# A fused cross-network recommender kernel: the second layer's steps reordered, one subtraction moved, gathers and prelude rearranged

## The reference

```
def _L0_rec_ref(inputs, w0, w1, w2, b0, b1, b2):
    x0 = inputs; xk = inputs; direct = []
    for idx, (W, b) in enumerate([(w0, b0), (w1, b1), (w2, b2)]):
        z = jnp.einsum('bhd,bkd,hks->bsd', x0, xk, W) + b[None, :, None]
        z = jax.nn.relu(z)
        if idx != 2:
            half = z.shape[1] // 2
            xk = z[:, :half, :]
            direct.append(z[:, half:, :])
        else:
            direct.append(z)
    return jnp.sum(jnp.concatenate(direct, axis=1), axis=-1)
...
    h = jnp.concatenate([z, dense_ctx], axis=1)
    h = jnp.maximum(h @ W_top1 + b_top1, 0.0)
    h = jnp.maximum(h @ W_top2 + b_top2, 0.0)
    y = h @ W_top3
```

## Time and profile before

| what | us |
|---|---|
| median of 3 runs | 2593.65 (2592.92 to 2595.34) |
| the profiled execution, its own time | 2598.07 |
| its span, first to last instruction | 2596.2 |
| PE busy | 2443.5 (94%) |
| DVE busy | 2169.6 (84%) |
| POOL busy | 1875.1 (72%) |
| ACT busy | 1661.3 (64%) |

### The profile page before, as it was taken

How to read it: one execution, slowest core, us unless ns; L and a number is a source line. 1 busy time by engine, 2 the same in 40 slices (tenths; PEclk the granted TensorE clock), 3 DMA queues, 4 the chain that set the end, 5 groups by cost and what they waited for, 6 DMA issues and landing times.

```text
span 2596.2 us, 32413 instructions
## 1 busy us (share of the span) xinstructions
PE 2443.5 (94%) x8654; PEld 1591.3 (61%) x8654; DVE 2169.6 (84%) x1872; ACT 1661.3 (64%) x2120; POOL 1875.1 (72%) x1270
## 2 busy tenths in 40 slices
PE   0899999999999999999999999999999999999989
PEld 0466666666656666666666666666666666666655
DVE  1588889889878888988988898898888888888880
ACT  1566666666666666766666676666666666666653
POOL 6578778777867777777787777778777777765450
PEclk6899999999999999999999999999999999999999
DMA  2677667667757766766776676677667666756730
GB/s 71 139 149 155 126 138 166 134 131 151 154 110 152 154 130 132 166 137 132 148 158 129 132 164 140 127 150 155 131 131 166 141 131 145 160 129 129 159 80 0
DMA packets 214715, 352.58 MB, mean 136 GB/s; under 512 B 34382, under 2 KB 47566, under 8 KB 214588
## 3 DMA queue, kind: packets, MB, share of 16 engines
q1 hardware_dynamic: 194717, 347.07, 61.6%
q0 software_dynamic: 19968, 5.15, 2.2%
HBM read 346.97 MB, written 5.12 MB: 136 GB/s over the span
## 4 chain that ended last, share of the span: by engine, by line
POOL 30%; issue 27%; PE 16%; DVE 9%; DMA 7%; ACT 7%; SPq 3%; POOLq 0%; ACTq 0%; DVEq 0%; another core or an unknown queue 0%
POOL emb L374 13%; POOL Pl L380 13%; DMA xb<-x_dram 7%; ACT Ph L514 5%; PE ps L807 5%; PE ps L797 4%; DVE P L692 3%; DVE ps L692 3%; PE ps L817 3%; POOL dir L404 3%; SPq L311 3%; DVE Pl L697 3%; PE ps L926 1%; PE ps L918 1%; POOL emb L385 1%
## 5 line engine op out<-in xcount | busy, mean ns | idle before, releaser
L380 POOL TENSOR_TENSOR Pl<-P,Ph 128x1024 fp32r<-128x1024 f32 x448 | 1072.3, 2397 | 479.1 <-ACT Ph L514 469.4
L692 DVE TENSOR_TENSOR P<-xb,ps 128x1024 f32<-128x1024 f32 x768 | 926.8, 1214 | 81.1 <-DMA xb<-x_dram 72.9
L807 PE MATMUL ps<-Ph,wh 128*128 128x512 f32 x1920 | 870.1, 459 | 8.1 <-ACT Ph L514 8.0
L697 DVE TENSOR_TENSOR Pl<-ps,Ph 128x1024 fp32r<-128x1024 f32 x512 | 626.1, 1223 | 178.9 <-ACT Ph L514 168.7
L374 POOL DMA_INDIRECT emb<-tbl_in,idx x624 | 601.0, 963 | 166.3 <-issue 145.3
L807 PE MATMUL ps<-Ph,wl 128*128 128x512 f32 x1792 | 707.4, 395 | 0.0
L514 ACT ACTIVATE Ph<-ps 128x1024 fp32r<-128x1024 f32 x512 | 523.3, 1022 | 285.3 <-DVE ps L692 217.3
L817 PE MATMUL ps<-Pl,wh 128*128 128x512 f32 x1920 | 689.7, 445 | 11.4 <-POOL Pl L380 11.3
L514 ACT ACTIVATE Ph<-P 128x1024 fp32r<-128x1024 f32 x448 | 474.6, 1059 | 325.3 <-DVE P L692 303.8
L692 DVE TENSOR_TENSOR ps<-xb,ps 128x1024 f32<-128x1024 f32 x512 | 628.2, 1227 | 28.1 <-DMA xb<-x_dram 10.2
L797 PE MATMUL ps<-P,wp 128*128 128x512 f32 x1280 | 603.7, 594 | 4.1 <-DVE P L692 4.1
(11 more groups left out here) (64 smaller groups left out, 826.7 us busy)
## 6 DMA issues: line engine op xcount, KB each, us to landing
xb<-x_dram SPq DMA_DIRECT2D x1280, 256.0 KB, 8.5
emb<-tbl_in,idx POOLq DMA_INDIRECT x624
x_dram<-rows_sb SPq DMA_DIRECT2D x64, 78.0 KB
xb<-w_in SPq DMA_DIRECT2D x15, 128.0 KB
xb<-wt_in SPq DMA_DIRECT2D x2, 512.0 KB, 8.6
xb<-dense_in SPq DMA_DIRECT2D x1, 768.0 KB, 5.9
wp<-w_in SPq DMA_DIRECT2D x5, 128.0 KB
xb<-w0a_in SPq DMA_DIRECT2D x1, 448.0 KB
```

What stands on the lines that cost most here:

```text
L380: pool.tensor_tensor(Pl[:, h_slot(ref, c, k)], P[:, p_slot(ref, c, k)], Ph[:, h_slot(ref, c, k)], ALU.subtract).then_inc(low_pool, 1)
L692: dve.tensor_tensor(p, xb[:, x], xk.unsqueeze(1).broadcast_to([128, 2, N]), ALU.mult)\
L697: dve.tensor_tensor(Pl[:, h_slot(ref, c, k)], p_ps, Ph[:, h_slot(ref, c, k)], ALU.subtract)\
L807: pe.matmul(z_of(c, k), w[:, q, j, :], Ph[:, h_slot(ref, c, k), j, :], start=k in (L1B, L2) and i + j == 0, stop=False)
```

## The change

1. `TURN`: layer 2 takes its pairs in layer 1's order (4 to 9, then 0 to 3), so each slot is used in the same turn by both layers, and SP refills it 10 steps before the next use (before: 6 steps for pairs 4 to 9). The two steps with the single 39th field are now 1 and 11.
2. `KIND`: steps 17 and 19 change kinds; step 17 is G and step 19, the last one, is P.
3. `REST_AT = 19`: DVE subtracts the rest of layer 0 right behind step 19's own work and not after two products of the next chunk; it has a semaphore of its own (`rest_ready`).
4. The gathers are listed step by step (`GATHERS`); the embeddings' full and low parts move from steps 15 and 17 to 17 and 18.
5. Prelude: PE runs 36 matmuls (`WARM`) into a bank that nobody reads, DVE takes `low_emb(0)` from POOL, layer 0's first group uses three banks, the rest form first.
6. The tower's staging tiles are moved to slots that are free earlier.

```diff
-KIND = "GVPVGPVGVPPGVGVGVPVG"
+WARM = 36
+KIND = "GVPVGPVGVPPGVGVGVGVP"
-REST_AT = 1
+REST_AT = 19
-HIGH_AT, FULL_AT, LOW_AT = 15, 15, 17
+HIGH_AT, FULL_AT, LOW_AT = 15, 17, 18
-SINGLE = 2 * PRE + 1
+SINGLE = 2 * PRE + 3
+TURN = [(i + PRE) % PAIRS for i in range(PAIRS)]
-GATHER_AT = [k for k in range(STEPS) if KIND[k] != "G"]
+NEXT_IDS_AT = (2, 0)
+GATHERS = [[1, 2, 3, 5, 9, 14, 16, 18, 19], [1, 2, 3, 5, 6, 8, 9, 10],
+           [1, 2, 3, 5, 6, 9, 10, 12, 14, 16, 18, 19], [1, 2, 3, 5, 6, 8, 9, 10, 18, 19]]
...
+        early_ps = (ps[:, 6, :], ps[:, 7, :], aux_ps, ps[:, 7, :], aux_ps, ps[:, 7, :], aux_ps)
...
-                    for p in range(PAIRS):
+                    for i, p in enumerate(TURN):
-                        sp.wait_ge(products, upto(T, ref, STEP, c, L2 + p))
+                        sp.wait_ge(products, upto(T, ref, STEP, c, L2 + i))
                         spread(c + 2 if p < PRE else c + 1, p)
...
-            low_emb(0)
-            early = 12
+            early = 13
...
-                x = x_slot(c, PRE + k) if k < L1B else x_slot(c + 1, k - L1B) if k < L2 else x_slot(c, k - L2)
+                x = x_slot(c + (L1B <= k < L2), TURN[k % PAIRS])
...
-                dve.tensor_tensor(sqx[LAST_LO, :], aux_ps[LAST_LO], sqx[LAST_LO, :], ALU.subtract).then_inc(aux_read, 1)
+                dve.tensor_tensor(sqx[LOWS, :], bank[LOWS], sqx[LOWS, :], ALU.subtract).then_inc(rest_ready, 1)
+            dve.wait_ge(emb_high, 1)
+            dve.tensor_tensor(emb2[:, :, 1, :], emb[:, :, :].rearrange("p f d -> p d f"),
+                              emb_h[:, :, :].rearrange("p f d -> p d f"), ALU.subtract).then_inc(emb_low, 1)
...
-                        if k == REST_AT and not end and not (first and c == 0):
-                            rest_low(T, c + 1)
+                        if k == REST_AT and not (last and c >= 2):
+                            rest_low(T, c + 2)
...
+            for i in range(WARM):
+                pe.matmul(z1_ps[:, 0], wp[:, 0, 0, :], wp[:, 0:2].rearrange("p q j m -> p (q j m)"), start=True, stop=True)
...
+            transposes(0)
+            pe.wait_ge(aux_read, 1)
+            for i, t in enumerate((FULL0, 0, 1)):
+                sums(t, early_ps[i])
+            for t in range(FULL0):
+                pe.wait_ge(aux_read, 2 + t)
+                contract0(t, 0, t == 0, False)
+                if t + 2 < FULL0:
+                    sums(t + 2, early_ps[t + 3])
+            pe.wait_ge(rest_ready, 1)
+            contract0(FULL0, 0, False, True)
```

More of the change, by code:

```diff
@@ L431, in tile @@
             def tile(T, ref, fields, first=False, last=False):
+                todo = [list(f) for f in fields]
                 for c in range(CPT):
[L434 to L437, removed]
                     for k in range(STEPS):
@@ L440, in tile @@
                             low(T, ref, c, k)
[L441 to L445, removed]
+                        if (c, k) == NEXT_IDS_AT and todo[2]:
+                            next_ids(T + 2)
+                        part = min(c, 1) if (c, k) < NEXT_IDS_AT else 2
+                        n = GATHERS[c].count(k) * (1 + (first and c == 0))
+                        for f in todo[part][:n]:
+                            gather(f)
+                        todo[part] = todo[part][n:]
                         if c == 0 and not first and k in FOLD1_AT:
@@ L463, in tile @@
                             low_emb(T + 1)
-            cuts = (0, 12, 21, 30, NF)
-            third, fourth, first, second = (range(a, b) for a, b in zip(cuts, cuts[1:]))
-            tile(0, 0, (range(early, 30), range(30, NF), third, fourth), first=True)
+            late, soon = len(GATHERS[0]), len(GATHERS[1])
+            cut = NF - late - soon
+            assert sum(map(len, GATHERS)) == NF
+            start, middle, rest = range(0, cut), range(cut, cut + late), range(cut + late, NF)
+            tile(0, 0, (range(early, cut + late), rest, start), first=True)
             with pool.Fori(1, TILES - 2) as T:
-                tile(T, 1, (first, second, third, fourth))
-            tile(TILES - 2, TILES - 2, (first, second, (), ()))
-            tile(TILES - 1, TILES - 1, ((), (), (), ()), last=True)
+                tile(T, 1, (middle, rest, start))
+            tile(TILES - 2, TILES - 2, (middle, rest, ()))
+            tile(TILES - 1, TILES - 1, ((), (), ()), last=True)
             pool.wait_ge(z2_read, chunks)
@@ L537, in _ @@
                 copy_x(0, AUX * g)
-                for t in range(T0):
-                    square(0, AUX * g + 1 + t, t)
-                    s = t - (T0 - PRE - 1)
+                if g:
+                    rest_squares(0, 1, AUX + 1)
+                for t in range(FULL0):
+                    square(0, AUX * g + 2 + t, t, aux_ps if g else early_ps[t + 1])
+                    if t == 0 and not g:
+                        rest_squares(0, 0, 1, early_ps[0])
+                    s = t - (FULL0 - PRE)
                     if g and 0 <= s < PRE and KIND[L1B + s] != "P":
@@ L708, in _ @@
             for s in range(PRE):
+                if s == 1:
+                    rest_low(0, 1)
                 dve.wait_ge(xb_in[s], 32)
@@ L851, in _ @@
             late = None
-            for g in range(2):
-                number = AUX * g
-                if g:
-                    pe.wait_ge(aux_read, number)
-                transposes(g)
-                for t in range(T0):
-                    pe.wait_ge(aux_read, number + 1 + t)
-                    sums(t)
-                    if t:
-                        contract0(t - 1, g)
-                    if g and t >= T0 - PRE:
-                        late = contract(0, 0, -1, L1B + t - (T0 - PRE), late)
-                pe.wait_ge(aux_read, AUX * (g + 1))
-                contract0(T0 - 1, g)
+            transposes(0)
+            pe.wait_ge(aux_read, 1)
+            for i, t in enumerate((FULL0, 0, 1)):
+                sums(t, early_ps[i])
+            for t in range(FULL0):
+                pe.wait_ge(aux_read, 2 + t)
[4 more added lines that the diff above has]
+            contract0(FULL0, 0, False, True)
+            transposes(1)
+            order = (FULL0, *range(FULL0))
+            for i, t in enumerate(order):
+                if i == 1:
+                    pe.wait_ge(rest_ready, 2)
+                else:
+                    pe.wait_ge(aux_read, READS + max(i, 1))
+                sums(t)
+                if i:
+                    contract0(order[i - 1], 1, i == 1, False)
+                if i >= T0 - PRE:
+                    late = contract(0, 0, -1, L1B + i - (T0 - PRE), late)
+            pe.wait_ge(aux_read, 2 * READS)
+            contract0(FULL0 - 1, 1, False, True)
             assert not late
```

74 lines of the change are left out of this document (41 added, 33 removed).

## The result

| what | before | changed |
|---|---|---|
| median of 4 runs | 2593.38 (2592.92 to 2595.34) | 2515.55 (2515.19 to 2517.52) |
| ratio, 95% interval | | 0.970 (0.9683 to 0.9717) |
| the profiled execution's span | 2596.2 | 2514.0 |
| start, up to the loop's first transposes | 100.3 | 97.9 |
| loop, from there to the last transposes (61 chunks) | 2319.4 | 2246.5 |

The changed kernel is 3.0% faster. The transposes run two chunks ahead of the steps, so the last ones stand at the start of the third last chunk; what the tables call the end has three chunks in it. Of the 82.2 us between the two profiled spans the loop has 72.9, the end 6.9 and the start 2.4. The medians differ by 77.8, since the profiled execution of before lay 4.7 us above its median.

The account below looks back on a forecast made before the run. PE was taken to bound the kernel, its gaps being what reordering can win. Terms 71 + 1 + 2 + 5 = 79 us off the 2593.65 us median gave 2515 us; range 2498 to 2547.

Parts of the forecast that it names:

- What bounds the kernel: PE, busy 94% of the span; its largest repeated gap is the wait for DVE at line 789, 55.0 us.
- The subtraction: Behind step 19: moving layer 0's rest subtraction there removes PE's wait, 1.23 us a chunk, 58 times, 71 us.
- The pair order: Layer 2's transfers: 10 steps of lead for 6 keep step 4's inputs on time for an earlier PE; costed at 0.
- rival 1: At step 4: PE meets late rounding or low part, losing about 0.5 us a chunk, 30 us; 2545 us, chance 0.15.
- The gathers: On POOL: three, not five, ahead of step 4's subtraction in chunk c = 1; mostly cover, 2 us (0 to 9).
- The last step plain: Last chunk, step 19 plain and 17 split: ACT rounds one product less ahead of the tower, 1 us (0 to 2).
- The prelude: Before the loop: 1.2 us for the transposes, some 2 for each of two groups; 5 us (0 to 16).
- rivals: The four alternative outcomes to the forecast, which itself had chance 0.66; the range takes in the first two only.
- Which clock: Prelude: added matmuls end at about 54 us, 8 us of nothing follow, half the clock expected at the first group.
- The second gap at step 8: Steps 5 to 8: a chain from PE through ACT ties PE and DVE once a chunk and stays whatever the change does.
- The bounds, 2500 to 2524: The forecast's own limits: prelude 16 or 0, POOL's waits 9 or 0, 58 gaps of 1.0 to 1.3 us.
- 2: Rival on the prelude: the added matmuls do keep the clock, 16 us for 5; 2504 us, chance 0.10.

Follow-up runs that it names:

- a_rest1: The changed kernel with the subtraction of layer 0's rest back at step 1 of the following chunk; 2587.04 us, ratio 0.9963.
- a_kind: The changed kernel with the old kinds of steps 17 and 19 (17 plain, 19 split on POOL); 2521.31 us, ratio 0.9715.
- a_gathers: The changed kernel with gathers as early as possible again, five ahead of step 4 in chunk c = 1; 2528.94 us, ratio 0.9739.
- a_warm0: The changed kernel without the 36 added matmuls of the prelude; 2518.57 us, ratio 0.9698.
- a_warm45: The changed kernel with 45 instead of 36 added matmuls in the prelude; 2514.56 us, ratio 0.9689.
- a_again: The changed kernel run again with nothing changed; 2517.84 us, ratio 0.969.
- a_early22: The changed kernel with 22 instead of 13 gathers ahead of the loop and single gathers in the first chunk; 2521.23 us, ratio 0.9705.

## Why the prediction was right, point by point

The forecast was 2515 us, the measured median 2515.55. The total is that close partly by luck: the largest term is right, and two small ones are off in opposite directions. And the 79 us were worked out on the profiled spans, which moved by 82.2, but taken off the median, which moved by 77.8.

- **What bounds the kernel** (PE's gaps, the one at line 789 first): right. a_rest1 gives the wait back and with it 68.9 us.
- **The subtraction, 1.23 us a chunk, 71 us:** right in the whole. The loop gained 72.9, 1.24 us by the median chunk. The added 0.17 and 0.11 us (hidden idle time, restart) were needed; the recorded 55.0 alone would have fallen short by 16. The spacings of the starts say the same: over 60 chunks of before, those ahead of and behind the contraction at line 789 are 70.2 us longer than two of 0.23 each.
- **The pair order at 0, as cover:** right in kind. It was the step on which most depended, and the runs price it: 28.5 to 30.9 us. I had put about half a us a chunk on losing it in rival 1, and that was the size (30 us).
- **The gathers, mostly cover, 2 us of POOL's waits:** PE's waits for POOL went from 11.3 to 9.9 us, 1.4 us. As cover they are worth up to 10.6 us, of which some 7 are the chunks c = 1 without POOL's pause.
- **The last step plain, 1 us (0 to 2):** undersized. It is 3.7 us in a_kind. What I had not looked for was POOL's last subtraction beside DVE's first of the tower. The end as a whole gained 6.9 us. Of these 2.9 lie ahead of the tower's first subtraction, in three chunks (101.3 us for 104.2), the first of which still has the wait at line 789 in before; 4.0 lie behind it. The other 3.2 were not taken apart in full. They are more than executions differ by here: the change, a_gathers, a_warm0, a_warm45, a_again and a_early22, which don't differ there but for gathers, all have 169.5 or 169.6.
- **The prelude, 5 us:** oversized. The transposes came 1.6 us sooner (61.92 for 63.55) and the first group won 3.2 us, but the second lost 2.5, and between executions the start varies by 7 us. That step assumed some 2 us for each group. Only the first uses three banks; the second still runs through the one bank, so its 2 us had no source, and with the rest form in front it takes longer: PE now waits for roundings there that it did not wait for before.
- **Which clock:** right. Full until 58.65, half at the transposes.
- **The second gap at step 8 "stays":** it stayed (DVE's wait there 1.89 before, 1.87 after), but I took it in the experiments for 0.5 us a chunk of PE's time. It was 0.17 for the median chunk.
- **The bounds, 2500 to 2524:** they don't follow from their terms. With each at its end (58 gaps of 1.0 or 1.3 us, 0 or 9, 0 or 2, 0 or 16) the sum is 58 to 102 us, and the time 2491 to 2536. The result doesn't hang on it.

Of the rivals, 1 is shown to be what happens without the cover. Of 2, the clock came in a_warm45, where PE is busy up to 0.9 us ahead of the transposes, but only for the first group (half again from 77.0 to 83.8), and not its 2504 us: 2514.56. 3 did not occur: PE waits for POOL 7 times, not 46. 4 neither. Each statement on the profile held: waits at line 806 none, PE 98% (97), transfers 1.6 us, 1.24 us a chunk (1.2), the first group 1.6 us sooner (1.2).

Open: why ACT stands for 3 to 8 us in some preludes. It was longest in the two kernels with 22 gathers issued early, but a_again, with 13, has 3.5 and 2.8 us too (its trace is of the slowest of its five executions), so the number of gathers isn't shown to be the cause. Open too are two pauses of POOL in all 14 traces, 4.5 to 7.1 us long, at the same two chunks of the loop, the 18th and the 41st. POOL in the changed kernel:

```profile
734.23 0.96 POOL L379 DMA_INDIRECT emb<-tbl_in,idx  x1 [4.76 <-issue]
...
1581.20 0.94 POOL L379 DMA_INDIRECT emb<-tbl_in,idx  x1 [5.91 <-issue]
```

These two chunks take 40.6 and 40.2 us, 7.7 us over the rest together; in before they took 43.6 and 39.2.

## What to carry to other kernels

Price a gap at the spacing of the instructions around it, not at the idle time that the profile records; and before moving what removes it, read who else is late within that distance behind it, for that slack is spent with it. Edits that by themselves remove no wait of PE (an order of transfers, an order of gathers) were worth 40 us here because they came with the one that did. Where the gap is beside a float32 matmul, compare with the same pair of instructions at a place without a wait before calling it one.

## What was new about the hardware

- A DVE subtraction of two SBUF tiles, 32 x 1024, took 2.58 us when it started 0.90 us after a POOL subtraction of 2.41 us (a_kind), and 1.22 us in the changed kernel, where no POOL subtraction ran beside it.
- The record behind a float32 matmul lasts 0.80 us and the next begins 0.64 us after it although nothing waited (1214.01 to 1214.65); elsewhere such matmuls are followed in 0.23. I read this as the float32 matmul still running under that record. Behind a wait the record lasts 0.50 us and the next follows in 0.33 to 0.34.
- Added matmuls kept the clock at full only as long as they ran on: with a pause of 7.3 us ahead of the transposes it was half there (the changed kernel), with 0.9 us it was full (a_warm45).
